# One tap of a dynamic filter moves from the tensor engine to GpSimd, and one closing sum from GpSimd to the vector engine

## What is computed

```python
out = zeros
for u in range(3):
    for v in range(3):
        patch = xp[:, :, u:u+56, v:v+56]                 # the padded, normalised x, shifted
        out = out + patch * cf[:, :, u, v][:, :, None, None] * sf[:, u*3+v][:, None]
x = x + out
```

## Time and profile before

| | us |
|---|---|
| median of 3 runs | 1646.33 |
| lowest and highest run | 1644.76, 1646.61 |
| the profiled execution | 1647.29 |
| its span, first to last instruction | 1645.5 |
| PE, DVE, ACT, GpSimd busy in the span | 1583.3, 1233.0, 1179.4, 1112.9 |

### The profile page before, as it was taken

How to read it: one execution, slowest core, us unless ns; L and a number is a source line. 1 busy time by engine, 2 the same in 40 slices (tenths; PEclk the granted TensorE clock), 3 DMA queues, 4 the chain that set the end, 5 groups by cost and what they waited for, 6 DMA issues and landing times.

```text
span 1645.5 us, 29770 instructions
## 1 busy us (share of the span) xinstructions
PE 1583.3 (96%) x10979; PEld 819.7 (50%) x10979; DVE 1233.0 (75%) x2338; ACT 1179.4 (72%) x2280; POOL 1112.9 (68%) x910
## 2 busy tenths in 40 slices
PE   4999999999998999999999999999999999999996
PEld 3457457457465344444444444444444444444442
DVE  5866866866856788888888888788888888888850
ACT  2054154154044699999999999999999999999984
POOL 1730720720722278888888888888888888888887
PEclk9999999999999799999999999999999999999999
DMA  2010210210225205100000600000410000000000
GB/s 86 1 40 40 70 39 40 70 40 39 70 33 126 89 2 85 44 13 13 12 13 13 117 12 13 13 12 13 66 59 17 13 12 13 12 8 7 7 7 12
DMA packets 15586, 57.21 MB, mean 35 GB/s; under 512 B 4560, under 2 KB 11088, under 8 KB 13008
## 3 DMA queue, kind: packets, MB, share of 16 engines
q1 hardware_dynamic: 15440, 55.31, 12.6%
HBM read 30.94 MB, written 24.22 MB: 34 GB/s over the span
## 4 chain that ended last, share of the span: by engine, by line
PE 86%; DVE 7%; POOL 3%; issue 2%; ACT 2%; DMA 0%; POOLq 0%; DVEq 0%; ACTq 0%
PE PS L1434 31%; PE PS L1368 16%; PE PS L1407 15%; PE PS L1301 7%; PE PS L1256 5%; PE PS L1246 3%; POOL accP L1162 2%; DVE st L507 2%; PE PS L1356 2%; DVE nmt L766 1%; PE PS L1344 1%; PE PS L1291 1%; PE PS L1290 1%; PE PS L1212 1%; PE PS L1421 1%
## 5 line engine op out<-in xcount | busy, mean ns | idle before, releaser
L759 DVE TENSOR_REDUCE nmt<-PS 128x1 f32<-128x448 f32 x1323 | 785.7, 620 | 188.0 <-PE PS L1368 187.4
L1162 POOL TENSOR_TENSOR accP<-accP,Pb 128x512 f32<-128x512 f32 x504 | 639.8, 1269 | 81.9 <-ACT Pb L1025 31.0
L1025 ACT ACTIVATE Pb<-PS 128x896 f32<-128x896 f32 (+1 forms) x700 | 627.2, 901 | 81.1 <-PE PS L1407 72.0
L990 ACT ACTIVATE PS<-PS,nmt 128x448 f32<-128x448 f32 x588 | 356.7, 607 | 18.9 <-DVE nmt L766 9.6
L1434 PE MATMUL PS<-Pb,VT 128*64 128x448 f32 x1400 | 322.7, 540 | 1.8 <-ACT Pb L1025 1.2
L1434 PE MATMUL PS<-Pb,xnf 128*64 128x448 f32 x1400 | 321.8, 538 | 0.0
L1368 PE MATMUL PS<-xnp,xin 96*64 96x448 bf16 x1408 | 250.0, 369 | 8.3 <-ACT PS L990 4.9
L1368 PE MATMUL PS<-Ka,Qa 96*64 96x448 bf16 x1372 | 242.4, 353 | 0.0
L1407 PE MATMUL PS<-xin,xnp 99*64 99x448 bf16 x1372 | 188.2, 351 | 0.7 <-ACT Pb L1025 0.6
L1407 PE MATMUL PS<-Qa,Ka 99*64 99x448 bf16 x1372 | 188.3, 352 | 0.0
L1368 PEld LDWEIGHTS PS<-xnp,xin 96*64 96x64 bf16 x1408 | 78.6, 111 | 138.6 <-ACT PS L990 50.4
(11 more groups left out here) (169 smaller groups left out, 1877.7 us busy)
## 6 DMA issues: line engine op xcount, KB each, us to landing
saved_v<-VT SPq DMA_DIRECT2D x4, 1600.0 KB, 11.3
xin<-in_x SPq DMA_DIRECT2D x4, 1568.0 KB, 6.7
saved_x<-xw SPq DMA_DIRECT2D x4, 1568.0 KB, 5.1
out<-xw SPq DMA_DIRECT2D x28, 224.0 KB, 1.9
saved_parts<-parts SPq DMA_DIRECT2D x4, 1176.0 KB, 8.0
xw<-saved_x SPq DMA_DIRECT2D x21, 224.0 KB, 2.6
xnf<-saved_v SPq DMA_DIRECT2D x2, 1600.0 KB, 17.0
VT<-saved_v SPq DMA_DIRECT2D x2, 1600.0 KB, 17.7
```

Source lines behind the costliest of these rows:

```text
L759: nc.vector.reduce_max(nmt[:, target % 2, b, t:t + 1], PS[0:BLK, bank, 0:CH], X, negate=True).then_inc(mx_free, 1)
L990: return nc.scalar.activation(PS[0:BLK, bank, 0:CH], PS[0:BLK, bank, 0:CH], ACT.Exp, bias=nmt[:, target % 2, b, t:t + 1], accum_out=sm[:, ...
L1025: nc.scalar.activation(Pb[:, j % PSLOTS, 0:m, :], PS[:, 2 * (k % 2):2 * (k % 2) + m, 0:CH], ACT.Exp).then_inc(exp_done, 1)
L1162: nc.gpsimd.tensor_tensor((accQ if j < TO_ACCP else accP)[:, :, REST:CH], (accQ if j <= TO_ACCP else accP)[:, :, REST:CH], Pb[:, j % PSLOT ...
```

## The change

GpSimd gets tap 4, the middle one: it now does five adds for each unit (1+3, +x, +4, +5, +7), and PE adds four taps, 0, 2, 6 and 8 (`BY_PE`). PE's `add_tap(u, 4)`, which stood behind the unit's last spread, is gone. The closing sum of unit 1 moves from GpSimd to DVE, between taps 6 and 7 of unit 2, where it reads `acc` and `part[2]`, both in SBUF (`POOL_UNITS` = 1: only unit 0's sum stays on GpSimd). ACT's copies stay. The counts that the waits need follow.

```diff
-PE_TAPS = TAPS // 2 + 1
-POOL_STEPS = 3
+BY_PE = (0, 2, 6, 8)
+PE_TAPS = len(BY_PE)
+POOL_STEPS = 4
+POOL_UNITS = 1
...
-                    if t % 2 == 0:
-                        dve.wait_ge(tap_added, PE_TAPS * k + t // 2 + 1)
+                    if t in BY_PE:
+                        dve.wait_ge(tap_added, PE_TAPS * k + BY_PE.index(t) + 1)
                     elif t < 7:
-                        dve.wait_ge(pool_step, POOL_STEPS * k + (1 if t < 5 else 3))
+                        dve.wait_ge(pool_step, POOL_STEPS * k + {1: 1, 3: 1, 4: 3, 5: 4}[t])
...
+                    if u < COPIED:
+                        dve.wait_ge(acc_copied, COPIED * g + u + 1)
                     nc.vector.tensor_tensor(xw[:, j * CH:(j + m) * CH].rearrange("p (h n) -> p h n", h=m),
-                                            PS[:, bank:bank + m, 0:CH], pu[:, 2, 0:m, :], ALU.add).then_inc(l0_done, 1)
+                                            acc[:, :, :] if u < COPIED else PS[:, bank:bank + m, 0:CH], pu[:, 2, 0:m, :],
+                                            ALU.add).then_inc(l0_done, 1)
...
-                        if t == 7 and u > COPIED:
+                        if t == 7 and u > POOL_UNITS:
                             l0_sum(u - 1)
...
-                    if 1 <= u <= COPIED:
+                    if 1 <= u <= POOL_UNITS:
                         l0_sum(u - 1)
                     pool.wait_ge(pool_step, POOL_STEPS * (k + 1) + 2)
+                    pool.wait_ge(prod_ready, TAPS * k + 5 + TAP_SLOTS)
+                    nc.gpsimd.tensor_tensor(part[0], part[1], prod[4][:, 0:m, :], ALU.add).then_inc(pool_step, 1)
+                    pool.wait_ge(pool_step, POOL_STEPS * (k + 1) + 3)
                     pool.wait_ge(prod_ready, TAPS * k + 6 + TAP_SLOTS)
-                    nc.gpsimd.tensor_tensor(part[0], part[1], prod[5][:, 0:m, :], ALU.add).then_inc(pool_step, 1)
-                    pool.wait_ge(pool_step, POOL_STEPS * (k + 1) + 3)
+                    nc.gpsimd.tensor_tensor(part[1], part[0], prod[5][:, 0:m, :], ALU.add).then_inc(pool_step, 1)
+                    pool.wait_ge(pool_step, POOL_STEPS * (k + 1) + 4)
                     pool.wait_ge(prod_ready, TAPS * k + 8 + TAP_SLOTS)
                     if u:
                         pool.wait_ge(l0_done, len(UNITS) * g + u)
-                    nc.gpsimd.tensor_tensor(part[2], part[0], prod[7][:, 0:m, :], ALU.add).then_inc(pooltaps, 1)
+                    nc.gpsimd.tensor_tensor(part[2], part[1], prod[7][:, 0:m, :], ALU.add).then_inc(pooltaps, 1)
...
                         if t in (4, 6):
                             add_tap(u, t - 4)
-                        elif t == TAPS - 1:
-                            add_tap(u, 4)
```

## The result

The changed kernel takes 1669.01 us, median of four executions, where the kernel before takes 1646.47: a ratio of 1.0139, interval 1.0116 to 1.0162. Slower was forecast; the forecast was 1662.7 and the range ended at 1668.0, so the median lies 1 us outside. The four executions are 1664.82, 1665.36, 1672.66 and 1672.91: a spread of 8 us that the kernel before (1644.76 to 1646.90) does not have. The traced execution took 1665.36, its span is 1663.5.

What follows compares the result with a forecast made beforehand. It took PE to pace the old filter and GpSimd's chain of dependent adds to end the new one: 6.0 us for that chain plus 10.4 for PE's falling clock, 16.4 over 1646.33, gives 1662.7 us; range 1651 to 1668.

Steps and rivals of the forecast that it cites:

- What bounds after the change: Filter: GpSimd's chain of dependent adds, 40.43 us in group 1, makes DVE's last sum late, 6.0 us in all.
- PE's gain: Filter: one add fewer for each unit saves 5.3 us of PE work per group, useful only if nothing else is late.
- the steps: Sign in the new profile: GpSimd's adds in group 1 follow each other at 2.17 us.
- the missing brackets: Sign: no bracket in GpSimd's timeline from unit 0's first add to unit 3's last, ending near 211.7.
- PE's busy time in the window: Sign: over the filter stretch it falls by about 5.3 us.
- DVE and GpSimd blocking each other: Unit 1's sum on DVE beside GpSimd's SBUF adds: 0 to 1.0 us per group, taken as 0 in the forecast.
- rival B: DVE and GpSimd keep each other waiting at unit 1's sum: up to 4.0 us, 1656.3 or 1666.7; chance 0.32.
- The clock: Behind the filter: PE's clock falls in its pauses; 2.6 us per group taken, 0 to 3.5 possible, 10.4 in all.
- PE's pauses: End of the filter: PE idles 2.4 us ahead of the last add and 3.1 us ahead of the mean.
- the seven fillers: Sign behind the filter: they take about 2.7 us in place of 1.48 if the clock falls.
- Rival A: The clock stays up and only GpSimd's chain costs: 1652.3 us; chance 0.18.
- Rival C: Not slower: GpSimd's adds follow closely enough, at steps below 2.09 us, to end in time: about 1644; chance 0.10.

Runs made afterwards that it cites:

- e1_fill: The changed kernel with more filler matmuls in PE's pauses at the end of the filter and ahead of the mean: 1655.78 us, ratio 1.0063.
- e2_psum: The changed kernel with unit 1's sum on DVE reading one operand from PSUM in place of the SBUF copy: 1668.61 us, ratio 1.0135.
- e6_after_again: The changed kernel itself, run once more without any edit for a second trace: 1659.35 us, ratio 1.0096.
- e3_psum_fill: The changed kernel with both more filler matmuls and unit 1's sum reading one operand from PSUM: 1652.70 us, ratio 1.0039.
- e4_tap_only_fill: The changed kernel with both closing sums (units 0 and 1) back on GpSimd, plus more filler matmuls: 1659.74 us, ratio 1.0083.

## Why the prediction was wrong where it was wrong

- **What bounds after the change: right.** GpSimd's start stays behind product 3, its adds follow at 2.17 and 2.04, and its end sets the last sum. 40.43 + 0.07 us were worked out for groups 1 to 3, 40.44 measured with the two other effects taken away, 6.1 us for the kernel where 6.0 stood. PE's gain was hidden whole: with the clock up (e1_fill) none of it came out in the time. Of the signs named, the steps and the missing brackets came as said; group 1's last sum starts 0.09 us behind the end of GpSimd's last add (213.15 + 1.13), though the profile names GpSimd as its releaser in group 0 alone and has "issue", no releaser found, in group 1; PE's busy time in the window fell by 3.6 us, not 5.3.
- **DVE and GpSimd blocking each other: put at 0 in the sum; it is 0.73 us in each group.** It stood as rival B with 0 to 1.0, and it happened in every group of every trace where the sum read two SBUF operands. The trace of before could not price it, since no such pair ran in it; the step that failed is taking the absence of a row for a price of 0. The sum waits out the rest of the add that it met (3.01 beside one that had just begun, 1.19 beside one that was nearly done), then the next add waits for the sum (2.81 and 2.82); with one operand in PSUM neither waits (1.08 and 2.08). So DVE and GpSimd meet in one place more than the semaphores, which the section on the core calls the only one. The Trainium skill states the rule ("SBUF — State Buffer", section "Who interferes with whom"): a DVE instruction with two SBUF inputs contends with a GpSimd instruction that reads SBUF, and whichever comes second blocks. These runs agree with it.
- **The clock: right in kind, wrong in size, and the range too narrow for it.** PE's pauses were forecast as 2.4 and 3.1 us and are 1.3 and 2.7, with one of 1.9 before them that the blocking brings (DVE's sum of unit 2 comes with GpSimd's end of the unit as forecast, but PE has its add of tap 6 later than I had it). The clock fell, and the seven fillers took 2.45 where I said 2.7. But the price was taken as 2.6 in each group, at most 3.5, from a stretch of 6.9 us at the start of group 0. The low clock doesn't end with the fillers: it reaches into the second layer's matmuls, which PE paces, and then costs up to 88.62 - 83.57 = 5.05 in a group (e2_psum; 4.71 in the changed kernel); in other groups, and in other executions of the same kernel, nothing. Sums over four groups in the traces: 9.1 and 2.6 for the changed kernel, 14.1 in e2_psum. The term was 10.4, within that, but its upper end was 14.0.
- **The median.** It lies 22.5 us above the kernel before, where 16.4 was forecast. 8.8 belong to the filters, taken as long as in the trace (6.0 forecast), so 13.7 are left against 10.4 for the clock: 2.8 of the miss is the blocking, 3.3 the clock. With the blocking alone put in, the forecast would have been 1665.6, the time of the traced execution (1665.36), in which 9.1 lie behind the filters. For the executions at 1673, which lift the median, the rest is put down to the clock by their granted clock alone, without a trace.
- **The range.** Its upper end, 1668, was B on top of the forecast, with the forecast's own middle price of the clock. Its own upper ends together, 6.0 + 4.0 + 14.0, would have given 1670.3, with the median inside; the measured ones, 6.0 + 2.9 + 4 x 5.05, give 1675.6, and the highest execution was 1672.9. The eight executions of the changed kernel lie from 1658.2 to 1672.9; six are within the range. Why the first four lie higher than the four of e6_after_again (medians 1669.01 and 1659.35) stays open; with the second four the median would have been inside.
- **Rival A (clock up) is e3_psum_fill**: 1652.7 against 1652.3 worked out. Rival C is out: no pair of dependent adds came closer than 2.14 us.

## What to carry to other kernels

Before work goes to an engine with idle time, look where in the stage that idle time lies and make the sum over its chain of dependent steps, from the moment it can start to the moment its result is wanted: GpSimd was a quarter idle in the old window and had room for one more add in unit 0, not for one in every unit. When an engine that was the pace gets relief, ask what it does in the pauses; here they cost, through TensorE's clock, up to 5.05 us in a group, where the work removed was 5.3 us and saved nothing. And a price that no row shows belongs into the range at both ends together with the others' ends, not only by itself.

## What the runs showed of the hardware that was not expected

The toll of a low clock varies from execution to execution of one and the same kernel: 0 to 4.71 us in a group of the changed kernel, 1658 to 1673 us in all, while the instructions ahead of it agree to 0.1 us. What it costs goes by where it lies: nothing while PE would have waited anyway (e6_after_again), all that PE's matmuls grow by where they set the pace. What decides when it falls stays open. And it can stay low while PE works without a pause, as in this window of e2_psum, where PE is busy 15.78 of 16 us and the granted clock reads 0.64:

```profile
218.00:234.00 16.00, 15.78 (x43) 7.84 (x43) 4.07 (x14) 6.79 (x11) 3.12 (x4) 0.64 0.02 9
```

Matmuls without a use, 27 for each group in e1_fill, kept it up in all four groups of that trace. They are no sure means: with the same fillers e4_tap_only_fill has a granted clock of 0.50 from 208.80 to 212.20, behind a pause of 1.61 us; it cost nothing there, since it is 83.57 from that group's last sum to the next first add.
